# Two-layer transformer on one core: GpSimd adds the attention masks for two steps in one operation, VectorE adds none

## The chip, the cores and the metric

One core of one Trainium2 chip. The metric is the device time of one execution in microseconds, as the median of several runs.

## The reference

x is 4 x 512 x 256 (B = 4 sequences). Layer 0 is a conditioned transformer block with 16 heads of width 16, an additive bias of 4 x 16 x 512 x 512 values in f32 (64 MB, the largest input) and a mask; layer 1 is a causal block with a gate. The part that the change touches:

```
scores = jnp.einsum('bhqd,bhkd->bhqk', q / math.sqrt(HEAD_DIM), k)
scores = scores + attention_bias
scores = jnp.where(src_mask, -jnp.inf, scores.astype(jnp.float32))
probs = jax.nn.softmax(scores, axis=-1).astype(v.dtype)
ctx = jnp.einsum('bhqk,bhkd->bhqd', probs, v)
```

## The kernel before

The work is written out by hand for each engine, with semaphores. Phases alternate: X(b) is the attention of layer 0 for sequence b+1 (b = -1 to 2), Y(b) that of layer 1 for sequence b. Beside each runs "dense" work (projections, feed-forward, norms) from other sequences, put in at slots that the table PLANS (L83) gives. In the trace X(-1) runs from about 45 to 147 us, X0 from 147 to 273, X1 from 374 to 495, X2 from 600 to 723.

A phase X has 64 steps, one for each head and query tile. Each step has a tile of 128 x 512 f32 in a ring of 12 (`tiles`, RING). Its life:

- SyncE loads the bias into it, `load_tile` (L385), once TensorE has read the tile of 12 steps before.
- The mask is added in place: `tile += mask_neg[:, t, :]`, where mask_neg (bf16, 128 x 4 x 512) holds one row block for each query tile t = `tile_of(s)[1]` and is rewritten for each sequence by VectorE, `turn_mask` (L1234), after all mask adds of the sequence before. GpSimd adds it, `add_mask` (L565, L572), 6 steps ahead (MASK_AHEAD). In the first phase, every fourth step is VectorE's instead (`masked_by_vector` L181, `add_mask` L1378, L1382), 16 steps in all.
- TensorE puts q.k into PSUM (L958), three steps ahead (AHEAD). VectorE adds it to the tile and takes the row maximum in one instruction, `add_bias` (L1384, L1391).
- The maximum is subtracted, by ScalarE (L696) or, every eighth step, by VectorE (`from_max`, L1398).
- TensorE transposes the tile (`turn`, L966), ScalarE takes the exponential (L705), TensorE multiplies with v (L979).

Steps 2i and 2i + 1 are the two query tiles t and t + 1 of one head, with t even, so their tiles lie side by side in the ring and their mask rows side by side in mask_neg.

GpSimd runs in order: in a phase X one mask at each slot, and behind it what falls due in that slot: `inv_std` (L575, L577: waits for VectorE's var_eps, then a power), row adds of 128 x 1024 (`add_row`, L580), and, in the first phase, a reordering of weights (L561). A norm goes: VectorE's statistics and var_eps (L1222), GpSimd's inv_std, VectorE's normalised tiles (`normalise`, L1292, four of 128 x 256; or `modulate`, L1300 and L1304), TensorE's transposes (`transposed`), which wait for them tile by tile. q and k are split into three bf16 parts by VectorE (`split`: L1358, L1362, L1365) and moved by DMA into the order of the scores (`to_roles`, L413). `gated` (L1342) is L1346 and L1348; L1348 frees a bank of PSUM for TensorE's feed-forward (L932). In phase Y GpSimd cuts diagonals (L611) and adds the first six masks of the next sequence but one (`first_masks`, L640); VectorE's `split_max` is L1416 to L1422.

Of the kernel before, what the change touches and what calls it, by code (L numbers as in the profile page):

```python
# [19 lines left out]
ALU = mybir.AluOpType  # L20
# [4 lines left out]
B, S, D = 4, 512, 256  # L25
# [28 lines left out]
STEPS = H * T  # L54
# [3 lines left out]
RING = 12  # L58
AHEAD = 3
MASK_AHEAD = 6  # L60
# [93 lines left out]
def s_no(l, b, i):  # L154
    return STEPS * place(l, b) + i
# [19 lines left out]
def tile_of(s):  # L175

    part, j = s // (2 * G), s % (2 * G) // 2
    return part // 2 * G + j, part % 2 * 2 + s % 2


def masked_by_vector(b, s):  # L181
    return b == 0 and s % 4 == 1


def masks(b, s, vector):

    return sum(masked_by_vector(c, i) == vector for c in range(b + 1) for i in range(s + 1 if c == b else STEPS))


def shifted_by_vector(s):  # L190
    return s % 8 == 3

# [32 lines left out]
def all_upto(streams, slot):  # L225
    for stream in streams:
        stream.upto(slot)


def the_rest(streams, slot):  # L230
    for s in range(slot, slot + 40):
        all_upto(streams, s)
    all_upto(streams, LAST)


def two_layers(nc, a, out):
# [21 lines left out]
    with ExitStack() as ctx:  # L258
        def sb(name, shape, dt=F32):
            return ctx.enter_context(nc.sbuf_tensor(name, shape, dt))  # L260
# [4 lines left out]
        def sem(name):  # L265
            return ctx.enter_context(nc.semaphore(name))
# [15 lines left out]
        mask_neg = sb("mask_neg", [P, T, S], BF16)  # L282
# [14 lines left out]
        tiles = sb("tiles", [P, RING, S])  # L297
# [44 lines left out]
        def tile(b, s):  # L342
            return tiles[:, (b * STEPS + s) % RING, :]
# [7 lines left out]
        w1_in, w2_in, wq_scaled = sem("w1_in"), sem("w2_in"), sem("wq_scaled")  # L351
        x_in, mask_in, mask_ready = [sem(f"x_in{b}") for b in range(B)], sem("mask_in"), sem("mask_ready")
        tile_in = [sem(f"tile_in{i}") for i in range(RING)]
        masked_p, masked_v, shifted_a, shifted_v = (sem(n) for n in ("masked_p", "masked_v", "shifted_a", "shifted_v"))
        s_filled, s_drained, e_filled, e_done = (sem(n) for n in ("s_filled", "s_drained", "e_filled", "e_done"))
        pv_done, raw_ready, raw_turned, ctx_normed, ctx_turned, ctx_ready = (sem(n) for n in (
            "pv_done", "raw_ready", "raw_turned", "ctx_normed", "ctx_turned", "ctx_ready"))
# [186 lines left out]
        def _(pool):  # L544
# [11 lines left out]
            def swap_columns(l):  # L556

                pool.wait_ge(qk_in[l], 16 * 2)
                for x, (w, scale) in enumerate(((wq, QSCALE), (wk, 1.0))):
                    yield 12 + 4 * x  # L560
                    pool.tensor_scalar(w[l][:, :, :].rearrange("p c (n d h) -> p (c n) d h", n=C, d=DH),  # L561
                                       raw[l][:, x, :, :].rearrange("p c (n h d) -> p (c n) d h", n=C, d=DH),
                                       scale, None, ALU.mult).then_inc(wq_scaled, 1)

            def add_mask(b, s):  # L565
                if masked_by_vector(b, s):
                    return
                n = b * STEPS + s
                if s == 0:
                    pool.wait_ge(mask_ready, b + 1)  # L570
                pool.wait_ge(tile_in[n % RING], 16 * (n // RING + 1))
                pool.tensor_tensor(tile(b, s), tile(b, s), mask_neg[:, tile_of(s)[1], :], ALU.add).then_inc(masked_p, 1)  # L572

            def inv_std(l, b, which):
                n = NORMS.index((l, b, which))  # L575
# [29 lines left out]
            def diagonal(b, h):  # L605

                pool.wait_ge(e_done, e_no(1, b, CHUNKS * (h + 1)))
                at = h % KEEP * P1
                for blocks in (prob[:, at:at + 2048].rearrange("p (i n) -> p i n", i=2)[:, :, 0:P],
                               prob[:, at + 512:at + 768].rearrange("p (i n) -> p i n", i=2)):  # L610
                    pool.affine_select(out=blocks, in_=blocks, compare_op=ALU.is_ge, fill=0.0, base=0,  # L611
                                       pattern=[[0, 2], [1, P]], channel_multiplier=-1).then_inc(diagonal_done, 1)
# [23 lines left out]
            def residual(b, at):  # L636
                yield at.x1
                set_x1(b)

            def first_masks(b, at):  # L640
                for s in range(MASK_AHEAD if b < B else 0):
                    yield at.masks + 2 * s
                    add_mask(b, s)

            def streams(at):
                return [Stream(second_norm(at)), Stream(projections(at))]
# [5 lines left out]
            inv_std(0, 0, 0)  # L652

            pool.wait_ge(norm_ready, T)
            for s in range(MASK_AHEAD):
                add_mask(0, s)
            def first_bo():
                yield 8
                add_bo(0)

            for kind, b in PHASES:
                dense = streams(PLANS[kind, b])
                if kind == "X":
                    if b < 0:
                        dense += [Stream(first_bo()), Stream(swap_columns(1))]
                    for s in range(STEPS):
                        if s + MASK_AHEAD < STEPS:
                            add_mask(b + 1, s + MASK_AHEAD)
                        all_upto(dense, s)
                    the_rest(dense, STEPS)  # L670
                    if b < 0:
                        for s in range(MASK_AHEAD):
                            add_mask(1, s)
                else:
                    dense += [Stream(residual(b, PLANS[kind, b])), Stream(first_masks(b + 2, PLANS[kind, b]))]
                    for slot in range(Y_SLOTS):
                        u, i = divmod(slot, 4)
                        if u >= LAG and i == 3:
                            diagonal(b, u - LAG)
                        all_upto(dense, slot)  # L680
                    the_rest(dense, Y_SLOTS)
# [504 lines left out]
        def _(dve):  # L1186
# [46 lines left out]

            def turn_mask(b, last):  # L1234
                if b:
                    dve.wait_ge(masked_p, masks(b - 1, STEPS - 1, False))
                    dve.wait_ge(masked_v, masks(b - 1, STEPS - 1, True))
                dve.wait_ge(v_step, last)
                for t in range(T):
                    ins = dve.tensor_scalar(mask_neg[:, t, :], mask_u8[:, t, :], -BIG, mask_row[:, 2, t:t + 1], ALU.mult, ALU.add)  # L1240
                ins.then_inc(mask_ready, 1)
# [133 lines left out]
                                  bv_all[l][:, :].rearrange("p (h d) -> p h d", d=DH).unsqueeze(1).to_broadcast([P, 2, H, DH]),  # L1375
                                  ALU.add).then_inc(drained_v, 1)

            def add_mask(b, s):  # L1378
                n = b * STEPS + s
                dve.wait_ge(mask_ready, b + 1)  # L1380
                dve.wait_ge(tile_in[n % RING], 16 * (n // RING + 1))
                dve.tensor_tensor(tile(b, s), tile(b, s), mask_neg[:, tile_of(s)[1], :], ALU.add).then_inc(masked_v, 1)  # L1382

            def add_bias(b, s):  # L1384
                n = s_no(0, b, s)
                if masked_by_vector(b, s):
                    dve.wait_ge(masked_v, masks(b, s, True))
                else:
                    dve.wait_ge(masked_p, masks(b, s, False))
                dve.wait_ge(s_filled, n + 1)  # L1390
                dve.tensor_tensor_reduce(tile(b, s), psS[:, n % 2, :], tile(b, s), 1.0, -3e38, ALU.add, ALU.max,  # L1391
                                         rmax[0][:, s:s + 1]).then_inc(s_drained, 1)

            def from_max(b, s):
                if not shifted_by_vector(s):
                    return
                dve.wait_ge(s_drained, s_no(0, b, s) + 1)
                dve.tensor_scalar(tile(b, s), tile(b, s), rmax[0][:, s:s + 1], -1.0, ALU.subtract, ALU.mult).then_inc(shifted_v, 1)  # L1398
# [106 lines left out]
            def phase_x(b, dense):  # L1505
                for s in range(-AHEAD, STEPS):
                    if 0 <= s + AHEAD < STEPS:
                        if s < 0 and masked_by_vector(b + 1, s + AHEAD):
                            add_mask(b + 1, s + AHEAD)
                        add_bias(b + 1, s + AHEAD)  # L1510
                    if 0 <= s + AHEAD - 1 < STEPS:
                        from_max(b + 1, s + AHEAD - 1)
                    if s >= 0 and s + AHEAD + 1 < STEPS and masked_by_vector(b + 1, s + AHEAD + 1):
                        add_mask(b + 1, s + AHEAD + 1)
                    if s >= 4 * G and s % (4 * G) == 8:
                        divide_by_sums(0, b + 1, s // (4 * G) - 1)
                    if s >= 0:
                        all_upto(dense, s)
                the_rest(dense, STEPS)
# [57 lines left out]
```

## Time and profile before

| | us |
|---|---|
| median of 3 runs | 988.09 |
| lowest, highest | 975.78, 990.17 |
| profiled execution | 990.58 |
| its span | 988.7 |
| mean granted TensorE clock | 0.926 |
| POOL L572, 240 mask adds | 283.4 busy, 1205 ns each |
| DVE L1382, 16 mask adds | 16.2 busy, 1010 ns each |
| DVE L1391, 256 biases with maximum | 174.3 busy, 688 ns each |

The profile is of one execution. PE is TensorE, DVE VectorE, ACT ScalarE, POOL GpSimd; L is a line of the kernel. An instruction's time begins when its waits on semaphores are over, so time that it stands for another reason is part of its duration. Where several instructions are merged into a row, its time is that from the first start to the last end.

### The profile page before, as it was taken

What the parts mean: (1) busy time and instruction counts of PE and PEld (TensorE: products, weight loads), DVE (VectorE), ACT (ScalarE), POOL (GpSimd) and SP (SyncE); (2) the same over time, 40 slices, a digit from 0 to 9 for tenths busy, and PEclk for the clock granted to TensorE, in tenths of its full rate; (3) what the DMA queues carried; (4) which work ended last, traced back from release to release, by engine and by line L of the source; (5) the groups of instructions that cost most, each with busy time, mean ns of one, the idle gap of its engine ahead of it and who ended that gap; (6) DMA issues with size and microseconds to landing.
All of it is one profiled execution on the core that took longest, in us unless ns stands there. A gap on an engine that the chain in (4) does not pass through costs nothing.

```text
span 988.7 us, 14633 instructions
## 1 busy us (share of the span) xinstructions
PE 827.4 (84%) x4856; PEld 494.6 (50%) x4856; DVE 599.9 (61%) x1693; ACT 493.0 (50%) x879; POOL 410.1 (41%) x421
## 2 busy tenths in 40 slices
PE   6778888789866879898998887899999898698778
PEld 2354456458542334575645443566656363445345
DVE  6599874774738936656847854656836654636021
ACT  1257785756701357577732455666742435054421
POOL 4377558755302447486302536486501123012320
PEclk7779999999976899999998997999999999899879
DMA  8776976434570036356741037455631126100000
GB/s 249 154 234 192 249 252 186 140 117 129 158 162 1 1 65 163 105 182 202 207 114 44 2 98 165 123 171 183 157 66 44 44 65 139 33 1 5 19 1 22
DMA packets 80045, 114.74 MB, mean 116 GB/s; under 512 B 7691, under 2 KB 43359, under 8 KB 79971
## 3 DMA queue, kind: packets, MB, share of 16 engines
q1 hardware_dynamic: 79971, 113.81, 41.8%
q8 instruction: 39, 0.64, 0.3%
q14 instruction: 35, 0.29, 0.1%
HBM read 86.33 MB, written 2.10 MB: 89 GB/s over the span
## 4 chain that ended last, share of the span: by engine, by line
PE 59%; DVE 19%; issue 8%; ACT 7%; DMA 3%; SPq 2%; POOL 1%; DVEq 0%; ACTq 0%; POOLq 0%
PE psD L932 11%; PE psD L944 11%; PE psE L966 6%; PE psC L979 5%; PE psD L904 4%; PE psC L1024 4%; PE psS L958 4%; PE psD L920 3%; DVE tiles L1391 3%; DMA qk<-work 2%; ACT tiles L696 2%; ACT prob L705 2%; DVE junk L1406 2%; PE psS L994 2%; PE psD L911 2%
## 5 line engine op out<-in xcount | busy, mean ns | idle before, releaser
L572 POOL TENSOR_TENSOR tiles<-tiles,mask_neg 128x512 f32<-128x512 f32 x240 | 283.4, 1205 | 97.3 <-DMA tiles<-in_fside_Bx16xSxS 79.4
L1391 DVE CUSTOM_DVE_ANT_0 tiles<-psS,tiles 128x512 f32<-128x512 f32 x256 | 174.3, 688 | 143.5 <-PE psS L958 129.9
L705 ACT ACTIVATE prob<-psE 128x512 f32<-128x512 f32 x256 | 150.9, 595 | 102.2 <-PE psE L966 94.6
L696 ACT ACTIVATE tiles<-tiles,rmax 128x512 f32<-128x512 f32 x224 | 161.4, 722 | 61.4 <-DVE rmax L1391 60.8
L966 PE MATMUL psE<-ident,tiles 128*128 128x128 f32 x1024 | 162.3, 282 | 7.7 <-ACT prob L705 7.3
L966 PEld LDWEIGHTS psE<-ident,tiles 128*128 128x128 f32 x1024 | 130.3, 145 | 63.5 <-ACT prob L705 25.0
L932 PE MATMUL psD<-hT,w 128*128 128x512 f32 x256 | 131.9, 627 | 17.4 <-DVE work L1348 13.6
L944 PE MATMUL psD<-w,work 128*128 128x256 f32 x512 | 133.8, 386 | 6.0 <-ACT hT L748 4.8
L1406 DVE CUSTOM_DVE_ANT_0 junk<-psS,later 128x128 bf16<-128x128 f32 x192 | 82.7, 444 | 86.4 <-PE psS L994 85.9
L611 POOL TENSOR_SCALAR_AFFINE_SELECT prob<-prob 128x256 f32<-128x256 f32 x128 | 52.4, 433 | 190.2 <-ACT prob L717 190.2
L958 PE MATMUL psS<-qk 96*128 96x512 bf16 x256 | 102.6, 403 | 31.9 <-DVE rmax L1391 20.6
L717 ACT ACTIVATE prob<-psE 128x512 f32<-128x512 f32 (+1 forms) x144 | 72.9, 532 | 90.2 <-PE psE L1012 89.4
L577 POOL TENSOR_TENSOR rstd<-var_eps,neg_half 128x4 f32<-128x4 f32 x16 | 16.5, 1033 | 226.8 <-DVE var_eps L1222 226.7
L944 PEld LDWEIGHTS psD<-w,work 128*128 128x128 f32 x512 | 92.0, 193 | 21.4 <-ACT hT L748 6.0
L994 PE MATMUL psS<-qk 96*128 96x128 bf16 x192 | 54.3, 296 | 28.0 <-DVE rmax L1406 18.0
L932 PEld LDWEIGHTS psD<-hT,w 128*128 128x128 f32 x256 | 44.8, 198 | 56.2 <-issue 33.7
L979 PE MATMUL psC<-prob,vx 128*32 128x256 f32 x1024 | 65.4, 399 | 1.0 <-ACT prob L705 1.0
L1406 DVE CUSTOM_DVE_ANT_0 junk<-psE,later 128x384 bf16<-128x384 f32 x64 | 39.4, 621 | 38.7 <-PE psE L994 38.6
L958 PEld LDWEIGHTS psS<-qk 96*128 96x128 bf16 x256 | 25.3, 99 | 65.4 <-DVE rmax L1391 32.3
L1024 PE MATMUL psC<-prob,vx 128*32 128x128 f32 (+3 forms) x512 | 48.4, 529 | 4.8 <-POOL prob L611 4.8
L1012 PE MATMUL psE<-qk 99*128 99x512 bf16 (+1 forms) x192 | 48.4, 306 | 2.4 <-DMA qk<-mT 1.5
L777 ACT ACTIVATE work<-psD,cols 128x512 f32<-128x512 f32 x32 | 22.0, 687 | 54.0 <-PE psD L932 54.0
(119 smaller groups left out, 1038.4 us busy)
## 6 DMA issues: line engine op xcount, KB each, us to landing
tiles<-in_fside_Bx16xSxS SPq DMA_DIRECT2D x256, 256.0 KB, 2.9
qk<-work SPq DMA_DIRECT2D x96, 256.0 KB, 5.8
w<-in_L_cond_W SPq DMA_DIRECT2D x12, 1024.0 KB, 5.5
res<-in_x SPq DMA_DIRECT2D x4, 512.0 KB, 4.8
out<-x SPq DMA_DIRECT2D x4, 512.0 KB, 2.8
mask_u<-in_mask_Bx1xSxS_bk SPq DMA_DIRECT2D x4, 256.0 KB, 5.5
qk<-mT SPq DMA_DIRECT2D x64, 3.0 KB
prob<-in_L_cond_W_ada SPq DMA_DIRECT2D x1, 512.0 KB
```

What stands on the lines that cost most here:

```text
L572: pool.tensor_tensor(tile(b, s), tile(b, s), mask_neg[:, tile_of(s)[1], :], ALU.add).then_inc(masked_p, 1)
L696: act.activation(tile(b, s), tile(b, s), ACT.Identity, scale=-1.0, bias=rmax[0][:, s:s + 1]).then_inc(shifted_a, 1)
L705: act.activation(prob0[:, part_no % 2, j, :, s % 2 * P:(s % 2 + 1) * P], psE[:, e_no(0, b, s) % 2, :].rearrange("p (k q) -> p k q", k=T), ...
L932: mm = pe.matmul(psD[:, n % 2, :], w1[:, c, f * P:(f + 1) * P], hT2[:, c, :], start=c == 0, stop=c == C - 1)
L944: mm = pe.matmul(psD[:, n % 2, t % 2 * D:(t % 2 + 1) * D], gT[:, f, t * P:(t + 1) * P], w2[:, f, :], start=f == 0, stop=f == FC - 1)
L958: pe.matmul(psS[:, n % 2, :], q6[0:ROWS, h, t * P:(t + 1) * P], k6[0:ROWS, h, :], start=True, stop=True).then_inc(s_filled, 1)
L966: mm = pe.transpose(psE[:, n % 2, kt * P:(kt + 1) * P], tile(b, s)[:, kt * P:(kt + 1) * P], ident[:, :])
L979: mm = pe.matmul(psC[j * QW:(j + 1) * QW, half * S // 2:(half + 1) * S // 2], vx[0][:, kt, at:at + QW], prob0[:, part_no % 2, j, kt, :], s ...
L994: pe.matmul(s_bank(n, i)[:, 0:(t + 1) * P], q6[0:ROWS, h, t * P:(t + 1) * P], k6[0:ROWS, h, 0:(t + 1) * P], start=True, stop=True).then_in ...
L1024: mm = pe.matmul(psC[j * QW:(j + 1) * QW, kt * P:S], vx[1][:, kt, VW * h:VW * h + QW], prob1[:, h % KEEP, P1_AT[kt]:P1_AT[kt] + S - kt * P ...
L1391: dve.tensor_tensor_reduce(tile(b, s), psS[:, n % 2, :], tile(b, s), 1.0, -3e38, ALU.add, ALU.max, rmax[0][:, s:s + 1]).then_inc(s_drained, 1)
L1406: dve.tensor_tensor_reduce(junk[:, n % 2, 0:w], s_bank(n, h * T + t)[:, 0:w], later[:, S - w:S], 1.0, -3e38, ALU.add, ALU.max, rmax[1][:, ...
```

## The change

VectorE's mask adds and their bookkeeping (`masked_by_vector`, `masks`, two semaphores) go. GpSimd's `add_mask(b, s)` becomes `add_masks(b, s)`, called for even s alone: it waits for both tiles of the pair and adds both masks in one operation of 128 x 2 x 512. One semaphore, `masked`, counts pairs; VectorE's bias waits for the count of its pair. Each pair is issued at the slot at which its first step's mask was issued.

```diff
-def masked_by_vector(b, s):
-    return b == 0 and s % 4 == 1
...
-            def add_mask(b, s):
-                if masked_by_vector(b, s):
-                    return
+            def add_masks(b, s):
+
                 n = b * STEPS + s
                 if s == 0:
                     pool.wait_ge(mask_ready, b + 1)
-                pool.wait_ge(tile_in[n % RING], 16 * (n // RING + 1))
-                pool.tensor_tensor(tile(b, s), tile(b, s), mask_neg[:, tile_of(s)[1], :], ALU.add).then_inc(masked_p, 1)
+                for i in range(2):
+                    pool.wait_ge(tile_in[(n + i) % RING], 16 * (n // RING + 1))
+                two, t = tiles[:, n % RING:n % RING + 2, :], tile_of(s)[1]
+                pool.tensor_tensor(two, two, mask_neg[:, t:t + 2, :], ALU.add).then_inc(masked, 1)
...
             def first_masks(b, at):
-                for s in range(MASK_AHEAD if b < B else 0):
+                for s in range(0, MASK_AHEAD if b < B else 0, 2):
                     yield at.masks + 2 * s
-                    add_mask(b, s)
+                    add_masks(b, s)
...
-            for s in range(MASK_AHEAD):
-                add_mask(0, s)
+            for s in range(0, MASK_AHEAD, 2):
+                add_masks(0, s)
...
                     for s in range(STEPS):
-                        if s + MASK_AHEAD < STEPS:
-                            add_mask(b + 1, s + MASK_AHEAD)
+                        if s % 2 == 0 and s + MASK_AHEAD < STEPS:
+                            add_masks(b + 1, s + MASK_AHEAD)
                         all_upto(dense, s)
...
                 if b:
-                    dve.wait_ge(masked_p, masks(b - 1, STEPS - 1, False))
-                    dve.wait_ge(masked_v, masks(b - 1, STEPS - 1, True))
+                    dve.wait_ge(masked, STEPS // 2 * b)
...
             def add_bias(b, s):
                 n = s_no(0, b, s)
-                if masked_by_vector(b, s):
-                    dve.wait_ge(masked_v, masks(b, s, True))
-                else:
-                    dve.wait_ge(masked_p, masks(b, s, False))
+                dve.wait_ge(masked, (STEPS * b + s) // 2 + 1)
...
             def phase_x(b, dense):
                 for s in range(-AHEAD, STEPS):
                     if 0 <= s + AHEAD < STEPS:
-                        if s < 0 and masked_by_vector(b + 1, s + AHEAD):
-                            add_mask(b + 1, s + AHEAD)
                         add_bias(b + 1, s + AHEAD)
                     if 0 <= s + AHEAD - 1 < STEPS:
                         from_max(b + 1, s + AHEAD - 1)
-                    if s >= 0 and s + AHEAD + 1 < STEPS and masked_by_vector(b + 1, s + AHEAD + 1):
-                        add_mask(b + 1, s + AHEAD + 1)
```

## Rows read from the trace of the kernel before

**Rows 1.** The page, part 1: busy time, share, instructions
```profile
PE 827.4 (84%) x4856; PEld 494.6 (50%) x4856; DVE 599.9 (61%) x1693; ACT 493.0 (50%) x879; POOL 410.1 (41%) x421
```

**Rows 2.** Windows: stretch, length, busy of PE, PEld, DVE, ACT, POOL, clock, DMA
```profile
45.00:150.00 105.00, 85.35 (x595) 52.19 (x594) 89.99 (x200) 75.90 (x134) 63.76 (x49) 0.91 0.79 232
385.00:500.00 115.00, 103.58 (x738) 69.70 (x736) 77.36 (x196) 78.78 (x134) 66.45 (x56) 1.00 0.59 177
```

**Rows 3.** The chain that ended last, 45 to 150 us, share by line
```profile
by line: ACT tiles L696 13.4%; issue 13.2%; ACT prob L705 9.9%; DVE tiles L1382 7.4%; DVE tiles L1391 6.4%; PE psE L966 5.9%; PE psD L904 5.4%; PE psC L979 5.3%; DVE res L1300 5.3%; PE psS L958 5.0%; DVE tiles L1398 3.4%; POOL tiles L572 3.
```

**Rows 4.** Groups by shape: busy us, mean ns, idle time before
```profile
L572 POOL TENSOR_TENSOR tiles<-tiles,mask_neg 128x512 f32<-128x512 f32 x240 | 283.4, 1205 | 97.3 <-DMA tiles<-in_fside_Bx16xSxS 79.4 <-DVE mask_neg L1240 7.9 <-DVE res L1304 7.5
L580 POOL TENSOR_TENSOR res<-res,b_all 128x1024 f32<-128x1024 f32 x4 | 9.4, 2352 | 7.3 <-DVE xh L1292 7.3
L1382 DVE TENSOR_TENSOR tiles<-tiles,mask_neg 128x512 f32<-128x512 f32 x16 | 16.2, 1010 | 0.0
```

**Rows 5.** Line L572: duration min/median/max in ns; who waited for it
```profile
L572 POOL TENSOR_TENSOR tiles<-tiles,mask_neg x240: 1143/1158/1617, 23.2 to 709.0; 128x512 f32<-128x512 f32 x120
...
  DVE tiles L1391: 12.9, 14
```

**Rows 6.** Groups of VectorE by shape
```profile
L1365 DVE TENSOR_TENSOR work<-work 128x512 bf16<-128x512 f32 x32 | 26.6, 832 | 0.4
L1398 DVE TENSOR_SCALAR tiles<-tiles,rmax 128x512 f32<-128x512 f32 x32 | 25.5, 798 | 0.0
...
L1292 DVE TENSOR_SCALAR xh<-res,mv,rstd 128x256 f32<-128x256 f32 x32 | 19.9, 663 | 1.1 <-POOL rstd L577 1.1
L1346 DVE TENSOR_SCALAR work<-work 128x512 f32<-128x512 f32 x32 | 19.3, 602 | 0.0
...
L1362 DVE CAST work<-work 128x512 bf16<-128x512 f32 x32 | 17.8, 556 | 0.4
...
L1300 DVE SCALAR_TENSOR_TENSOR res<-res,mv,ada 128x256 f32<-128x256 f32 x16 | 10.9, 720 | 1.5 <-ACT ada L755 1.3
```

**Rows 7.** Two lines of VectorE, ns min/median/max
```profile
L1292 DVE TENSOR_SCALAR xh<-res,mv,rstd x32: 402/452/1258, 180.6 to 817.9; 128x256 f32<-128x256 f32 x32
...
L1398 DVE TENSOR_SCALAR tiles<-tiles,rmax x32: 482/712/1458, 50.1 to 716.2; 128x512 f32<-128x512 f32 x32
```

**Rows 8.** Order of time at the start: start us, us
```profile
29.86 0.43 DVE L1362 CAST work<-work 128x512 bf16<-128x512 f32 x1
30.19 5.57 POOL L572 TENSOR_TENSOR tiles<-tiles,mask_neg 128x512 f32<-128x512 f32 x4 [2.46 <-DMA res<-in_L_cond_Wk]
...
30.33 1.56 DVE L1365 TENSOR_TENSOR work<-work 128x512 bf16<-128x512 f32 x1
...
33.22 1.53 DVE L1365 TENSOR_TENSOR work<-work 128x512 bf16<-128x512 f32 x1
...
37.93 0.69 DVE L1365 TENSOR_TENSOR work<-work 128x512 bf16<-128x512 f32 x1
```

**Rows 9.** Order of time, modulation: undisturbed, then in the first phase
```profile
19.67 0.88 DVE L1300 SCALAR_TENSOR_TENSOR res<-res,mv,ada 128x256 f32<-128x256 f32 x2 [1.01 <-ACT ada L755]
...
59.78 3.54 DVE L1300 SCALAR_TENSOR_TENSOR res<-res,mv,ada 128x256 f32<-128x256 f32 x2 [0.25 <-ACT ada L755]
63.35 2.55 DVE L1304 SCALAR_TENSOR_TENSOR res<-res,rstd,ada 128x256 f32<-128x256 f32 x2
```

**Rows 10.** Order of time around the norm in X1
```profile
459.60 0.71 DVE L1398 TENSOR_SCALAR tiles<-tiles,rmax 128x512 f32<-128x512 f32 x1
...
460.85 1.82 DVE L1292 TENSOR_SCALAR xh<-res,mv,rstd 128x256 f32<-128x256 f32 x2
...
463.20 1.80 DVE L1292 TENSOR_SCALAR xh<-res,mv,rstd 128x256 f32<-128x256 f32 x2
...
458.87 11.62 POOL L572 TENSOR_TENSOR tiles<-tiles,mask_neg 128x512 f32<-128x512 f32 x10
```

**Rows 11.** The chain at the start of X0: start us, us
```profile
145.55 3.39 POOL tiles L572 x3
```

More of the change, by code:

```diff
@@ L178, in tile_of @@
     return part // 2 * G + j, part % 2 * 2 + s % 2
-def masked_by_vector(b, s):
-    return b == 0 and s % 4 == 1
-def masks(b, s, vector):
-    return sum(masked_by_vector(c, i) == vector for c in range(b + 1) for i in range(s + 1 if c == b else STEPS))
 def shifted_by_vector(s):
@@ L353, in two_layers @@
         tile_in = [sem(f"tile_in{i}") for i in range(RING)]
-        masked_p, masked_v, shifted_a, shifted_v = (sem(n) for n in ("masked_p", "masked_v", "shifted_a", "shifted_v"))
+        masked, shifted_a, shifted_v = (sem(n) for n in ("masked", "shifted_a", "shifted_v"))
         s_filled, s_drained, e_filled, e_done = (sem(n) for n in ("s_filled", "s_drained", "e_filled", "e_done"))
@@ L671, in _ @@
                     if b < 0:
-                        for s in range(MASK_AHEAD):
-                            add_mask(1, s)
+                        for s in range(0, MASK_AHEAD, 2):
+                            add_masks(1, s)
                 else:
@@ L1376, in keep_values @@
                                   ALU.add).then_inc(drained_v, 1)
[L1378 to L1382, printed above, removed]
             def add_bias(b, s):
                 n = s_no(0, b, s)
-                if masked_by_vector(b, s):
-                    dve.wait_ge(masked_v, masks(b, s, True))
-                else:
-                    dve.wait_ge(masked_p, masks(b, s, False))
+                dve.wait_ge(masked, (STEPS * b + s) // 2 + 1)
                 dve.wait_ge(s_filled, n + 1)
```

## The prediction

> **What bounds the kernel now.** I read the page first, for the engines' shares: TensorE is busy for 827 of 989 us, VectorE for 600, GpSimd for 410 [rows 1]. So no engine's total is the limit by itself, and the stages have to be read apart. The windows over two phases X (layer 0's attention, the only place where masks are added) show two regimes [rows 2]. In the first one, 45 to 150 us, VectorE is busy for 90 of 105 us and GpSimd for 64; TensorE has 20 us of gaps. In a later one, 385 to 500 us, TensorE is busy for 104 of 115 us, VectorE for 77, GpSimd for 66. The chain of work in the first phase [rows 3] passes through ScalarE (L696 and L705, 23%) and VectorE; VectorE's own mask adds, L1382, are 7.4% of these 105 us, 7.8 us. Third come the groups of GpSimd and VectorE by shape [rows 4, 6], for the price of each operation, and last the order in time at the places where both engines work at once [rows 8 to 11].
>
> **What the rows show of the two engines side by side.** L1398, whose shortest run is 482 ns, takes up to 1458 [rows 7]. 1458 less the 300 ns that are left of it is one mask add of 1158 [rows 5]: the instruction stood until GpSimd's was over, then ran. L1300 takes 0.44 us undisturbed (two in 0.88, rows 9) and 1.77 each where a 2.35 us GpSimd add lies over them [rows 9]. L1292, L1346, L1362, L1365, L1300 and L1304 show the same; L1391, which reads PSUM, keeps to its time. When GpSimd has a backlog the two take turns: in X1 four L1292 take 1.82 + 1.80 us beside ten adds in a row of 11.62 us [rows 10]. From means less the undisturbed duration this costs VectorE: L1398 32 x (798-482) = 10.1 us, L1292 32 x (663-402) = 8.4, L1346 32 x (602-430) = 5.5 (floor as L1362's, of the same width), L1365 32 x (832-690) = 4.5, L1362 32 x (556-430) = 4.0, L1300 16 x (720-440) = 4.5: 37 us, of which mask adds are the greater part [rows 6 to 9].
>
> **The change part by part.**
> *Price of a pair.* Before shows no 128x1024 add of f32 and bf16. Nearest: the one-tile add, 1205 ns in the mean, 1158 median [rows 4, 5], so 2.32 to 2.41 a pair, and L580, as wide with two f32 inputs, 2352 [rows 4]. I take 2.35. 2 x 1158 is 2316, so nothing is saved by joining. [...]
> *GpSimd's load.* 240 singles become 128 pairs: 283.4 us become 128 x 2.35 = 301. All 17 us fall in the first phase (64 to some 81 of 105 us); elsewhere it is unchanged. GpSimd waits there for tiles and for norms, so this hides; without cover it would be 17 us.
> *VectorE's sixteen L1382 go*: 16.2 us at 1010 ns [rows 4], all in the first phase. On the chain are 7.8 of them [rows 3]; ScalarE's two lines stand right behind, so I credit the chain's share: **-7.8** (bounds -16.2, all of it, and -4, if ScalarE takes the place in half).
> *The start.* GpSimd's first masks lie beside the four splits of q and k, which end in the load that the first scores wait for. Before, two L1365 take 1.56 and 1.53 instead of 0.69 [rows 8]. After, pairs run 23.2-25.6-27.9-30.3-32.6-35.0-37.3 without a gap (the wait for Wk, 2.46 us, falls under the third). L1362 at 29.86 stands until 30.3, L1365 until 32.6, the next L1362 until 35.0, and L1365 until 37.3: the second split ends at 37.6 instead of 34.75, and this is serial: **+2.9** (bounds 0 and 3.2).
> *First phase, modulation.* The pairs of L1300 and L1304 take 3.54 and 2.55 us instead of 0.88 each, one GpSimd operation over each [rows 9]. One of these operations is 2.35 long already, the others are masks. With pairs each of the others is up to 1.2 longer; two or three of them count. Add the splits and L1398 of the phase. I take **+4** (bounds 0 and +9, three quarters of a doubling of what L1300, L1304, L1365, L1362 and L1398 lose there).
> *Start of X0.* mask_neg is rewritten, and steps 0 to 2 wait for GpSimd one add each, 3.39 us on the chain [rows 11]. After, step 0 waits for 2.35 and the third tile for the second pair, 4.7: **+1.2**.
> *The norms inside the phases.* inv_std frees both engines at once: GpSimd starts on the masks that it held back, VectorE on L1292. This happens four times (two norms in X0, one each in X1 and X2; L1292's largest is 1258 for a floor of 402, rows 7). X1, walked through: pairs from 458.87 end at 461.2, 463.6, 465.9. L1398 at 459.60 stands until 461.2, a bias step follows, the first L1292 ends at 463.9, the second at 466.2, a bias step, the last two near 469; before they ended at 465.0 [rows 10]: +4. TensorE's transposes wait for exactly these, and it is the full engine there. The same walk gives +1.5 at X0's first norm, where two pairs are ready and then L580 waits itself for L1292; +3 at its second, with three pairs; and +1.7 in X2, where the fourth pair's tiles have not landed. Sum **+10** (bounds 0 and 13).
> *L1346, L1398, L1362 and L1365 in X0 to X2.* A wait met at random grows from half of 1.16 us to half of 2.35. These lose about 16 us there now, so 16 more in all; L1346 stands ahead of the operation that frees TensorE's bank (L1348), the others have two steps of slack. I put a fifth on the path: **+3.5** (bounds 0 and 16).
> *Mask latency.* The first tile of a pair is ready one tile's arrival and 1.2 us later. Before, only 14 of 256 steps waited for a mask, 12.9 us in all [rows 5], nearly all counted above. 0. The last phases and phase Y have few masks, beside split_max: **+1**. Semaphores: two waits on tile_in before each pair instead of one before each single, same count.
>
> Sum: -7.8 + 2.9 + 4 + 1.2 + 10 + 3.5 + 1 = **+14.8**. The profiled execution took 990.6 us and would take 1005; it lies 2.5 above the median of 988.1, so against the median I predict **1003 us**.
>
> **The rivals.**
> *Relief wins (the other side).* If TensorE's and ScalarE's queues absorb the longer stands, the norms' +10 and the +3.5 vanish, since L1391 has idle time before it in every phase, and the first phase keeps its -7.8: 988.1 - 7.8 + 2.9 + 4 + 1.2 + 1 = 989; with all 16.2 of L1382 and no loss by turns, 972. For it: VectorE is busy for only 61% of the span. Against: the L1292 stand right before the transposes of a TensorE that is 90% busy. It decides from where the four norm places lose under 2 us together.
> *The turns cost in full.* If each of the 37 us doubles and all is on the path, in place of the +4, +10 and +3.5: 988.1 - 7.8 + 2.9 + 1.2 + 37 + 1 = 1022. Against: L1398's wait appears in front of nobody for long, and an engine in order with idle time gives some back.
> *GpSimd lets VectorE in between the two halves of a pair.* Then a stand is as before, and the sum is 988.1 - 7.8 + 1.2 = 982. Against: L1300 stood through a 2.35 us add as one piece [rows 9]. The Trainium skill (SBUF — State Buffer, section "SBUF: two separate sides") says the shared port pair is held for a whole instruction; this trace agrees, 1.77 us each where 0.44 is the floor.
> *Masks come late.* If each of the 14 waits grows by the 1.2 us of the second tile, that is +17 beside the sum: 1020. Against: load, mask and use are several steps apart; for it: the first tiles after each norm are taken at once.
>
> **How the numbers follow.** Chances: the forecast, 994 to 1012, 0.50; relief wins, 980 to 993, 0.25; between the halves, 0.03; turns in full, 1012 to 1022, 0.15; masks late, 0.07. Range 980 to 1018: it leaves out about 0.1 above and the 0.05 below. Two per cent, about what can be told from no change, is 19.8 us: slower than 1007.9 has the rivals above, 0.22 less a little, and a tenth of the forecast: 0.30. Faster than 968.3 needs all of L1382 and a faster run besides: 0.04. The rest, 0.66.
>
> **What would show it.** In the profile after: the pair at 2.35 us with 128 of them; GpSimd at about 427 us busy; L1382 gone; mean L1398 near 1.1 us and L1292 (from res) near 1.0, with maxima of 2.65; the first scores near 47.5 instead of 44.6; at the four norms TensorE waiting for L1292 by 2 to 4 us more. It is wrong if the L1292 and L1398 maxima stay at 1.26 and 1.46, if a pair is far from 2.35, or if VectorE waits for L572 far beyond 12.9 us.

## The result and the profile after

| | before | after |
|---|---|---|
| median, us (lowest to highest, 4 runs each) | 985.41 (975.78 to 990.17) | 1006.54 (1001.87 to 1009.11) |
| profiled execution, its span | 990.58, 988.7 | 1007.85, 1006.1 |

(The 988.09 us given ahead of the prediction are the median of the first three of these four runs.) The changed kernel is slower: ratio 1.0214, 95% interval 1.016 to 1.0267, so about 21 us. That is clear of no change, though the interval does not clear 2%. Ratios compare only the runs within 1.5% of a kernel's fastest, medians are of all its runs, so the two can differ a little. Between the two profiled executions it is 17.3 us. The line numbers move: GpSimd's add is now L564, the bias L1373, from_max L1380, normalise L1283, gated L1337 and L1339, split L1353 and L1356.

The page after, part 1, the line that answers to [rows 1]:

```profile
PE 837.5 (83%) x4856; PEld 501.4 (50%) x4856; DVE 614.8 (61%) x1677; ACT 494.6 (49%) x879; POOL 403.4 (40%) x309
```

TensorE has the same 4856 matmuls and is busy for 10 us more (827.4 before); its mean granted clock is 0.919 instead of 0.926. VectorE has 16 instructions less and is busy for 15 us more (599.9 before). GpSimd has 112 instructions less and is busy for 7 us less. So GpSimd's sum fell, VectorE's own work fell by 16 us, and its busy time rose all the same. The groups by shape say where (busy us, mean ns | idle time before), beside [rows 4, 6]:

```profile
L564 POOL TENSOR_TENSOR tiles<-tiles,mask_neg 128x1024 f32<-128x1024 f32 x128 | 276.5, 2177 | 114.5 <-DMA tiles<-in_fside_Bx16xSxS 102.7 <-DVE res L1295 6.0 <-DVE mask_neg L1231 5.8
...
L1373 DVE CUSTOM_DVE_ANT_0 tiles<-psS,tiles 128x512 f32<-128x512 f32 x256 | 174.3, 687 | 140.8 <-PE psS L950 133.3 <-POOL tiles L564 6.9
L1380 DVE TENSOR_SCALAR tiles<-tiles,rmax 128x512 f32<-128x512 f32 x32 | 38.1, 1192 | 0.0
L1356 DVE TENSOR_TENSOR work<-work 128x512 bf16<-128x512 f32 x32 | 27.8, 869 | 0.4
...
L1283 DVE TENSOR_SCALAR xh<-res,mv,rstd 128x256 f32<-128x256 f32 x32 | 25.4, 836 | 1.1 <-POOL rstd L569 1.1
...
L1337 DVE TENSOR_SCALAR work<-work 128x512 f32<-128x512 f32 x32 | 23.8, 742 | 0.0
...
L1353 DVE CAST work<-work 128x512 bf16<-128x512 f32 x32 | 21.2, 661 | 0.4
```

from_max went from 798 to 1192 ns in the mean, normalise from 663 to 836, gated's first operation from 602 to 742, split's cast from 556 to 661. The bias, which reads PSUM, stayed at 688 and 687. The standing is the time that an instruction takes beyond its floor, the duration that it has undisturbed. With the floors of the prediction the standing of the six groups named there rose from 37 to 65 us (32 x 710 + 32 x 434 + 32 x 312 + 32 x 179 + 32 x 231 + 16 x 326 ns). VectorE waited less for masks than before (6.9 us, 12.9 in [rows 5]).

Single lines, ns min/median/max, beside [rows 5, 7]: the largest stand grew by 0.84 us (1458 to 2302 ns), the add by 0.98.

```profile
L564 POOL TENSOR_TENSOR tiles<-tiles,mask_neg x128: 2120/2137/2569, 22.6 to 723.3; 128x1024 f32<-128x1024 f32 x128
```
```profile
L1380 DVE TENSOR_SCALAR tiles<-tiles,rmax x32: 475/1400/2302, 51.2 to 731.8; 128x512 f32<-128x512 f32 x32
```

Where the time went is read from the bias steps of each phase, first and last start in us: L1391 of before, windows on the four phases X,

```profile
L1391 DVE CUSTOM_DVE_ANT_0 tiles<-psS,tiles x64: 673/691/693, 45.4 to 143.2; 128x512 f32<-128x512 f32 x64
L1391 DVE CUSTOM_DVE_ANT_0 tiles<-psS,tiles x64: 674/691/693, 146.8 to 267.8; 128x512 f32<-128x512 f32 x64
L1391 DVE CUSTOM_DVE_ANT_0 tiles<-psS,tiles x64: 672/691/693, 374.1 to 491.6; 128x512 f32<-128x512 f32 x64
L1391 DVE CUSTOM_DVE_ANT_0 tiles<-psS,tiles x64: 673/691/693, 600.0 to 719.5; 128x512 f32<-128x512 f32 x64
```

and L1373 of after:

```profile
L1373 DVE CUSTOM_DVE_ANT_0 tiles<-psS,tiles x64: 672/691/692, 47.2 to 143.9; 128x512 f32<-128x512 f32 x64
L1373 DVE CUSTOM_DVE_ANT_0 tiles<-psS,tiles x64: 673/691/693, 148.4 to 270.3; 128x512 f32<-128x512 f32 x64
L1373 DVE CUSTOM_DVE_ANT_0 tiles<-psS,tiles x64: 674/691/693, 377.6 to 504.3; 128x512 f32<-128x512 f32 x64
L1373 DVE CUSTOM_DVE_ANT_0 tiles<-psS,tiles x64: 673/691/693, 611.9 to 734.4; 128x512 f32<-128x512 f32 x64
```

The lag, after less before at the same step, is 1.8 us at the first bias and 0.7 at the end of the first phase: the relief and the losses there nearly cancel. X0 takes it to 2.5, X1 from 3.5 to 12.7, X2 from 11.9 to 14.9. X1 is the largest single piece, 9.2 us, and it is made of two things: VectorE's stands, and TensorE's clock behind them. The first growth, 1.1 us, is a stand away from any norm. A pair starts as soon as its tiles have landed, and gated's first operation starts 0.12 us behind it and takes 2.30 us, where the same one took 1.24 before (order of time, start us, us; first VectorE, then GpSimd):

```profile
400.93 2.30 DVE L1337 TENSOR_SCALAR work<-work 128x512 f32<-128x512 f32 x1
```
```profile
400.81 2.14 POOL L564 TENSOR_TENSOR tiles<-tiles,mask_neg 128x1024 f32<-128x1024 f32 x1 [1.04 <-DMA tiles<-in_fside_Bx16xSxS]
```

Over the next steps, 16 to 19, the lag grows by 2.25 us more, from 4.8 to 7.0. One L1337 stands for 0.6 us there; the rest goes with the clock. Windows of before and of after over these same steps, and of the stretch at 1.2 GHz inside the second (stretch, length, busy of PE, PEld, DVE, ACT, POOL, clock, DMA):

```profile
404.69:411.10 6.41, 4.82 (x23) 2.65 (x22) 4.46 (x11) 3.60 (x7) 0.31 (x1) 1.00 0.31 84
```
```profile
409.47:418.13 8.66, 6.50 (x23) 3.35 (x22) 5.03 (x12) 3.61 (x7) 1.32 (x1) 0.80 0.23 67
412.60:416.00 3.40, 3.40 (x9) 1.57 (x7) 1.30 (x3) 1.21 (x2) 0.00 (x0) 0.50 0.07 19
```

The same 23 matmuls take 4.82 us before and 6.50 after. The granted clock fell to 1.2 GHz at 412.6, after ten microseconds in which TensorE had been busy for 6.4; in before it stayed at 2.4 GHz over the same steps. The inv_std at 420 then releases two pairs at once, and L1380 and L1337 take 1.96 and 1.75 us beside them (0.98 and 0.65 before), but this puts only 0.5 us on the lag (7.0 to 7.5).

The other place is the norm that the prediction walked through [rows 10]:

```profile
467.09 1.70 DVE L1380 TENSOR_SCALAR tiles<-tiles,rmax 128x512 f32<-128x512 f32 x1
...
469.31 1.94 DVE L1283 TENSOR_SCALAR xh<-res,mv,rstd 128x256 f32<-128x256 f32 x2
...
471.78 4.21 DVE L1283 TENSOR_SCALAR xh<-res,mv,rstd 128x256 f32<-128x256 f32 x2
```
```profile
466.36 4.42 POOL L564 TENSOR_TENSOR tiles<-tiles,mask_neg 128x1024 f32<-128x1024 f32 x2
471.59 4.25 POOL L564 TENSOR_TENSOR tiles<-tiles,mask_neg 128x1024 f32<-128x1024 f32 x2 [0.81 <-DMA tiles<-in_fside_Bx16xSxS]
```

The second two normalised tiles take 4.21 us instead of 1.80, two whole pairs. Counted from var_eps (457.63 before, 465.12 after) the last one ends 3.5 us later than before. The lag grows by 4.0 us up to step 48, and by 1.0 more up to step 50, while the clock is at 1.2 GHz (474.0 to 480.8). Windows over steps 44 to 50, before, then after:

```profile
459.00:469.99 10.99, 9.06 (x76) 5.80 (x74) 7.97 (x19) 8.36 (x14) 10.99 (x10) 1.00 0.65 220
```
```profile
466.48:482.45 15.97, 11.67 (x76) 7.18 (x74) 11.52 (x18) 8.47 (x14) 10.10 (x5) 0.79 0.45 146
```

So the clock is part of the loss in the profiled execution. From the mean clocks of the two, TensorE was at 1.2 GHz for an estimated 146 us of before and 163 us of after (1 less the mean clock, times two, times the span). In the two places shown, the drop follows a stretch in which TensorE had waited; that the stands caused it is likely from this order of events, but no run shows it by itself.

### The profile page after: what moved, and what is told of

It reads as the page before. It is cut to its first block, busy times and chain, and to the rows that moved or that the text cites. A ratio compares the mean times of both kernels' runs of the same rounds, so it can differ in the third digit from the quotient of the medians.

```text
span 1006.1 us, 14613 instructions
## 1 busy us (share of the span) xinstructions
PE 837.5 (83%) x4856; PEld 501.4 (50%) x4856; DVE 614.8 (61%) x1677; ACT 494.6 (49%) x879; POOL 403.4 (40%) x309
## 4 chain that ended last, share of the span: by engine, by line
PE 59%; DVE 20%; issue 8%; ACT 6%; DMA 3%; SPq 2%; POOL 1%; DVEq 0%; ACTq 0%; POOLq 0%
PE psD L924 11%; PE psD L936 11%; PE psE L958 7%; PE psS L950 4%; PE psC L971 4%; PE psD L896 4%; PE psC L1016 4%; PE psD L912 3%; DVE tiles L1373 3%; PE psD L903 2%; DMA qk<-work 2%; DVE junk L1388 2%; PE psS L986 2%; DVE xh L1283 2%; PE psD L882 2%
## 5 line engine op out<-in xcount | busy, mean ns | idle before, releaser
L564 POOL TENSOR_TENSOR tiles<-tiles,mask_neg 128x1024 f32<-128x1024 f32 x128 | 276.5, 2177 | 114.5 <-DMA tiles<-in_fside_Bx16xSxS 102.7
L1373 DVE CUSTOM_DVE_ANT_0 tiles<-psS,tiles 128x512 f32<-128x512 f32 x256 | 174.3, 687 | 140.8 <-PE psS L950 133.3
L958 PE MATMUL psE<-ident,tiles 128*128 128x128 f32 x1024 | 163.9, 284 | 10.8 <-ACT prob L697 9.2
```

Of the source, the lines that this page charges most:

```text
L564: pool.tensor_tensor(two, two, mask_neg[:, t:t + 2, :], ALU.add).then_inc(masked, 1)
L958: mm = pe.transpose(psE[:, n % 2, kt * P:(kt + 1) * P], tile(b, s)[:, kt * P:(kt + 1) * P], ident[:, :])
```

## The experiments

The theory ("hold"): the VectorE operations named above, which read and write SBUF alone, stand until GpSimd's running one is over, and a pair nearly doubles the time for which it runs (1158 to 2137 ns). Rivals: "load" (GpSimd has 16 masks more in the first phase), "mask latency" (the first tile of a pair is ready later). The rival that the traces add is the clock: after's four runs had a mean granted clock of 0.919 to 0.928, the 49 recorded runs of before 0.918 to 0.944. Each ratio below is to the kernel before, run beside it on the same chip.

**1. Singles, all by GpSimd.**

```diff
 def masked_by_vector(b, s):
-    return b == 0 and s % 4 == 1
+    return False
```

> The kernel before, with the sixteen mask adds of VectorE in the first phase given to GpSimd as single adds of 128x512; no pairs. If the longer hold of a pair is what cost time (theory 'hold'), this kernel is not slower: VectorE loses 16.2 us of work and meets singles only, 980 to 988 us, and from X0 on it is like before. If it is GpSimd's greater load in the first phase ('load'), this carries all of that and shows most of the loss: about 1000.

984.37 us, ratio 0.9948 (0.9923 to 0.9973). GpSimd's load of the first phase is carried here in full (301.4 us of mask adds) and the kernel is slightly faster than before, so "load" is out, and the relief of VectorE is worth half a per cent net.

**2. Two singles in place of a pair.**

```diff
+                for i in range(2):
+                    ins = pool.tensor_tensor(tile(b, s + i), tile(b, s + i), mask_neg[:, tile_of(s + i)[1], :], ALU.add)
+                    ins.then_inc(masked, 1)
-                two, t = tiles[:, n % RING:n % RING + 2, :], tile_of(s)[1]
-                pool.tensor_tensor(two, two, mask_neg[:, t:t + 2, :], ALU.add).then_inc(masked, 1)
```

The waits of VectorE count twice as far.

> The changed kernel, but add_masks issues two adds of 128x512, one after the other, in place of one of 128x1024. Order, waits for both tiles and the pair's semaphore count stay as in the changed kernel. 'Hold': VectorE gets in between the two, so most of the loss is gone: 985 to 993 us, L1292 of X1 and X2 back under 1.3 us. 'Mask latency' (the first tile of a pair is ready later) or 'load': it stays near 1005.

991.45 us, ratio 1.002 (0.998 to 1.006). Order, waits and the moment at which VectorE may go on are those of the changed kernel; only that each pair is two GpSimd operations instead of one differs, and 1.9 of the 2.1% are gone by the ratios, 15 us by the medians. The granted clock does not account for it: it was 0.911 to 0.927 in this kernel's runs, as low as in the changed kernel's. from_max and the bias in this kernel, groups by shape:

```profile
L1374 DVE CUSTOM_DVE_ANT_0 tiles<-psS,tiles 128x512 f32<-128x512 f32 x256 | 174.2, 688 | 158.0 <-PE psS L951 126.2 <-POOL tiles L564 31.3
...
L1381 DVE TENSOR_SCALAR tiles<-tiles,rmax 128x512 f32<-128x512 f32 x32 | 22.2, 694 | 0.0
```

from_max is back at 694 ns. VectorE now waits for masks, 31.3 us against 16.3 in kernel 1. The distance between kernels 1 and 2 is 0.7%. It may be the price of the later mask of a pair, but it comes together with a lower clock, 0.921 in the mean against 0.932. In the 49 recorded runs of the kernel before, 0.01 of clock goes with some 7.4 us (a straight line through them), so that an estimated 8 us would go with this difference alone; what lowered the clock is open. So the change in parts, by ratios: -0.5% relief, +1.9% hold, and +0.7% that goes with the order of the pairs and is not explained further. The first and the last are each near the width of their intervals; the hold is not.

**3 and 4. GpSimd waits at six norms** until the four tiles are normalised, in the changed kernel and in the one before.

```diff
                 pool.tensor_tensor(rstd[:, :], var_eps[:, :], neg_half[:, :], ALU.pow).then_inc(rstd_ready, 1)
+                if (l, b, which) in ((0, 0, 1), (1, 0, 0), (1, 0, 1), (1, 1, 0), (1, 1, 1), (1, 2, 0)):
+                    pool.wait_ge(norm_ready, T * (n + 1))
```

> The changed kernel, and GpSimd, after inv_std of the six norms inside X0, X1 and X2 that end in L1292, waits until the four tiles are normalised before it goes on with masks. 'Hold' has half of the loss at these places: L1292 falls to 0.41 us each, and the time to 994 to 1000. If the norms are not where it is lost, it stays at 1006 or rises by the delay of the masks (up to +4).

1015.26 us, ratio 1.0258 (1.0192 to 1.0325).

> The kernel before with the same wait at the six norms. Singles cost less there: 'hold' gives 2 to 7 us, 981 to 986 of 988, the delayed masks could eat that. If masks get late, 990 or more.

1002.94 us, ratio 1.0142 (1.01 to 1.0183). Kernel 3 lies above every range given for it; kernel 4 fell where the expectation put late masks, and further out. normalise did fall to its floor, but the masks came late, in kernel 3 too (34.6 us of waiting for them); kernel 4, groups by shape:

```profile
L1393 DVE CUSTOM_DVE_ANT_0 tiles<-psS,tiles 128x512 f32<-128x512 f32 x256 | 174.7, 688 | 146.7 <-PE psS L960 110.1 <-POOL tiles L572 35.6
...
L1294 DVE TENSOR_SCALAR xh<-res,mv,rstd 128x256 f32<-128x256 f32 x32 | 11.7, 412 | 1.1 <-POOL rstd L577 1.1
```

The wait for masks grew from 12.9 to 35.6 us while the standing of L1292 that it removed was 8 us. GpSimd's backlog after a norm is itself wanted soon; it cannot be put off by the 4 us that a norm takes. Late masks are not all of it in kernel 4: one from_max there stood for 5.84 us, in a row of eleven adds of 128x512 without a gap (its line's min/median/max, then order of time, VectorE and GpSimd):

```profile
L1400 DVE TENSOR_SCALAR tiles<-tiles,rmax x32: 481/622/5840, 49.6 to 718.1; 128x512 f32<-128x512 f32 x32
```
```profile
670.63 5.84 DVE L1400 TENSOR_SCALAR tiles<-tiles,rmax 128x512 f32<-128x512 f32 x1
```
```profile
663.86 12.33 POOL L572 TENSOR_TENSOR tiles<-tiles,mask_neg 128x512 f32<-128x512 f32 x11
```

**5. Half tiles:** kernel 1 with two adds of 128x256 for each tile.

```diff
+                for x in range(2):
+                    half = slice(x * S // 2, (x + 1) * S // 2)
+                    ins = pool.tensor_tensor(tile(b, s)[:, half], tile(b, s)[:, half], mask_neg[:, tile_of(s)[1], half], ALU.add)
+                    ins.then_inc(masked_p, 1)
-                pool.tensor_tensor(tile(b, s), tile(b, s), mask_neg[:, tile_of(s)[1], :], ALU.add).then_inc(masked_p, 1)
```

> GpSimd adds all masks, each tile's in two adds of 128x256: the hold is half of a single's, the number of operations is four times that of the pairs, and GpSimd's total grows by about 0.18 us for each extra operation (2 x 1158 - 2137), 46 us. 'Hold': VectorE's stands shrink further (L1398 under 0.7 in the mean instead of 0.75) and the time is 980 to 985 where singles gave 984, unless GpSimd's total makes masks late in the first phase; then up to 992. If only the number of handovers counted, it would be worse than pairs, above 1006.

1009.68 us, ratio 1.018, with a wide interval (1.0011 to 1.0348): the four runs spread from 995.79, the profiled one, to 1016.6. The median is where I had put "only the number of handovers counts". This goes against "hold" as I had put it, and the trace says why. from_max by shape, its line's min/median/max, and one of its places in order of time (VectorE, then GpSimd):

```profile
L1400 DVE TENSOR_SCALAR tiles<-tiles,rmax 128x512 f32<-128x512 f32 x32 | 54.7, 1709 | 0.0
```
```profile
L1400 DVE TENSOR_SCALAR tiles<-tiles,rmax x32: 480/538/10822, 47.4 to 721.5; 128x512 f32<-128x512 f32 x32
```
```profile
100.11 10.82 DVE L1400 TENSOR_SCALAR tiles<-tiles,rmax 128x512 f32<-128x512 f32 x1
```
```profile
98.71 11.94 POOL L574 TENSOR_TENSOR tiles<-tiles,mask_neg 128x256 f32<-128x256 f32 x19
```

The median is 538 ns, as short holds should give. But five of the 32 stood for 5.8 to 10.8 us, beside an unbroken row of GpSimd adds, and ended as the row ended. TensorE waited for from_max for 17.8 us in all. Here the two engines did not take turns. So the length of one operation is not all; a row of short ones can shut VectorE out altogether. With singles of 1.16 us this is rarer: the one of kernel 4 is the only such case in the traces of the kernels with singles (largest L1398 1458 before, 1477 in kernel 1). GpSimd's sum also rose, to 340.5 us, from 301.4 in kernel 1.

**6. Four tiles in one add,** from the changed kernel, issued eight steps ahead.

```diff
-                two, t = tiles[:, n % RING:n % RING + 2, :], tile_of(s)[1]
-                pool.tensor_tensor(two, two, mask_neg[:, t:t + 2, :], ALU.add).then_inc(masked, 1)
+                four = tiles[:, n % RING:n % RING + 4, :].rearrange("p (j i) k -> p j (i k)", i=2)
+                t = tile_of(s)[1]
+                rows = mask_neg[:, t:t + 2, :].rearrange("p i k -> p (i k)").unsqueeze(1).to_broadcast([P, 2, 2 * S])
+                pool.tensor_tensor(four, four, rows, ALU.add).then_inc(masked, 1)
```

> Four tiles in one add of 128x2048 (some 4.1 us), issued eight steps ahead. 'Hold' carried on from singles to pairs (+15 to +20 us a doubling): L1398 beyond 1.8 us in the mean, 1020 to 1045 us, part of it by masks that come late, to be read from L1391's wait for the mask. If hold is not the cause, near 1000.

1070.29 us, ratio 1.09 (1.079 to 1.101), beyond my range. The add takes 4105 ns:

```profile
L566 POOL TENSOR_TENSOR tiles<-tiles,mask_neg 128x2048 f32<-128x2048 f32 x64 | 262.4, 4105 | 253.4 <-DMA tiles<-in_fside_Bx16xSxS 238.4 <-DVE mask_neg L1233 8.2 <-DVE res L1297 6.9
...
L1382 DVE TENSOR_SCALAR tiles<-tiles,rmax 128x512 f32<-128x512 f32 x32 | 60.6, 1893 | 0.0
```

GpSimd's mask time is the least of all kernels that add masks, 262 us, and the kernel is the slowest. GpSimd now sits idle for 238 us until tiles land: with four tiles of twelve tied together the ring is a bound of its own. How much of the 9% is that and how much the hold was not separated.

**7 and 8. Eight steps ahead** instead of six (`MASK_AHEAD = 8`), in kernel 1 and in the changed kernel.

> All masks by GpSimd as singles, issued eight steps ahead instead of six. GpSimd then does two more masks in the time in which it waits for a norm's var_eps, so fewer are left to collide with L1292. 'Hold': 1 to 4 us less than the 984 of six ahead. If the norms' collisions do not matter, 984; if GpSimd waits for tiles that have not landed and inv_std comes late, 988.

987.65 us, ratio 1.004 (0.9988 to 1.0092).

> The changed kernel with pairs issued eight steps ahead. 'Hold': a pair less to collide at each norm, 2 to 6 us less than 1006. Otherwise 1006, or more where inv_std is late behind a tile that has not landed.

1009.46 us, ratio 1.0252 (1.0129 to 1.0375). No gain in either. In kernel 8 normalise fell to 555 ns in the mean, as meant, and from_max rose to 1432: the collisions moved to another operation.

```profile
L1380 DVE TENSOR_SCALAR tiles<-tiles,rmax 128x512 f32<-128x512 f32 x32 | 45.8, 1432 | 0.0
...
L1283 DVE TENSOR_SCALAR xh<-res,mv,rstd 128x256 f32<-128x256 f32 x32 | 16.4, 555 | 1.1 <-POOL rstd L569 1.1
```

**9. No masks.** Both engines' adds left out, the bias waits for the tile's load.

```diff
             def add_mask(b, s):
-                if masked_by_vector(b, s):
-                    return
+                return
...
-                if masked_by_vector(b, s):
-                    dve.wait_ge(masked_v, masks(b, s, True))
-                else:
-                    dve.wait_ge(masked_p, masks(b, s, False))
+                dve.wait_ge(tile_in[(b * STEPS + s) % RING], 16 * ((b * STEPS + s) // RING + 1))
```

> The kernel before without any mask add: GpSimd's and VectorE's are both left out, the bias step waits for the tile's load alone (so masked keys are not masked). It measures what all mask adds cost on the path, relief and turns together. 'Hold': more than VectorE's own 8 us come back, 965 to 975 of 988, and L1292, L1398, L1346 fall to their floors. If the masks were hidden and only VectorE's sixteen cost time: 980.

961.88 us, ratio 0.9724 (0.9658 to 0.9789). It is below the 965 to 975 that I had expected of "hold". The masks cost 2.8% in the kernel before, though GpSimd is busy for only 41% of it; the changed kernel pays 4.9 points. from_max and normalise stand at their floors:

```profile
L1391 DVE TENSOR_SCALAR tiles<-tiles,rmax 128x512 f32<-128x512 f32 x32 | 15.4, 482 | 0.0
L1288 DVE TENSOR_SCALAR xh<-res,mv,rstd 128x256 f32<-128x256 f32 x32 | 11.7, 411 | 1.1 <-POOL rstd L576 1.1
```

**10. Pairs, and every subtraction of the maximum by ScalarE** (`shifted_by_vector` returns False).

> The changed kernel with VectorE's 32 subtractions of the maximum (L1380, 1192 ns in the mean, 22 us of it standing) given to ScalarE (32 x 0.72 us more there). If these stands are on the path, 997 to 1002 of 1006; if they are off it and ScalarE's load takes their place, 1006 to 1012.

1002.25 us, ratio 1.0112 (1.0057 to 1.0166). By the ratios half of the change's loss goes with VectorE's 32 operations, by the medians (1006.54 and 1002.25, taken beside different runs of before) a fifth, in spite of 23 us more for ScalarE. So their standing is on the path in part, some 4 to 10 us.

**11. Pairs from the second sequence on,** the first phase as before.

```diff
+                if b:
+                    if s % 2 == 0:
+                        for i in range(2):
+                            pool.wait_ge(tile_in[(n + i) % RING], 16 * (n // RING + 1))
+                        two, t = tiles[:, n % RING:n % RING + 2, :], tile_of(s)[1]
+                        pool.tensor_tensor(two, two, mask_neg[:, t:t + 2, :], ALU.add).then_inc(masked_p, 1)
+                    return
```

> The kernel before in the first phase (singles, VectorE's sixteen), pairs as in the changed kernel for the sequences 1 to 3. The trace puts +0.7 us of the change into the first phase and the rest behind it. So about 1004, at least 1.5% above before. If the loss came from the first phase after all (start, load, modulation), 990.

1006.76 us, ratio 1.0166 (1.0104 to 1.0228). Most of the loss is there without any change to the first phase, in line with the lags of the bias steps.

**12. Kernel 1 with holds at X0's two norms** (the diff of 3 with its first two entries alone).

> All masks by GpSimd as singles (984) and, at the two norms of X0 alone, GpSimd waits until the four tiles are normalised. The run with holds at six norms gained 4.8 us in X0 by its trace and lost them in X1 and X2, where masks came late. So 979 to 981; if that gain was only a shift that is given back at the next wait, 984 or more.

985.27 us, ratio 0.997 (0.9917 to 1.0023). Not to be told from kernel 1: whatever the holds gain in X0 does not last to the end. Kernel 1 remains the fastest that computes everything, 0.5% below the kernel before.

## Why the prediction was right

The likeliest time was 1003 and the measured one 1006.5, and the main mechanism named, VectorE standing for as long as one GpSimd operation lasts, is the one that the runs show. That the sum came so close is in part luck: some terms were too large, one was too small, and TensorE's clock was not among them. By its steps:

- **The stand until GpSimd's operation is over.** Right. Kernel 2 changes this alone and takes 1.9 of 2.1% back; kernel 9 removes it and finds the floors. One reading behind it was loose: in [rows 9] the two L1300 did not take 1.77 us each. The view of that line gives 1.38 and 2.24, the second beside the 2.35 us add, and a floor of 0.48 (two records overlap in 0.88). The point holds by the second one.

```profile
L1300 DVE SCALAR_TENSOR_TENSOR res<-res,mv,ada x2: 1380/1808/2235, 59.8 to 61.9; 128x256 f32<-128x256 f32 x2
```

- **Price of a pair.** 2.35 was too high; it is 2137 in the median, 2177 in the mean. 2 x 1158 less 2137 is 179 ns saved by joining, where the prediction had nothing. The nearest row had two f32 inputs, this one has f32 and bf16, and the row's own 512-wide form was not in the trace: I compared the width of one operation with that of another. GpSimd's total was 403 instead of 427 us for the same reason.
- **VectorE's sixteen adds, -7.8, start +2.9, modulation +4.** Together -0.9 at the end of the first phase; measured +0.7. The start alone was +1.8. L1353 and L1356 stood for 2.35 and 2.49 us, but the next pair ran out a little sooner than walked. So the relief and the modulation together gave back 1.1, not the 3.8 of the sum.
- **Start of X0, +1.2.** The lag grew from 0.7 to 1.6 at the first bias, but was 0.9 from step 5 on: +0.2 that lasted.
- **The norms, +10.** X1's walked one put 4.0 on the lag of the bias steps, as worked out. X0's first put on 0.9 (1.5 worked out; gone four steps later, where before has a stretch at 1.2 GHz of its own, 187.0 to 190.4), its second 2.1 (3), X2's 0.9 (1.7). That is 7.9 directly. Behind X0's second and X1's the lag grew by another 1.7 and 1.0 over stretches at 1.2 GHz.
- **L1346, L1398 and splits, +3.5.** This is the term that was mis-sized. I took random meetings, doubled, with a fifth on the path. L1398 (L1380) met a pair in 21 of its 32 places, with a median of 1400 ns where 712 was before, and its standing rose from 10.1 to 22.7 us, more than double. Right behind an inv_std lie six of these stands, 6.7 us; twelve, 12.3 us, lie beside pairs that had started when their tiles landed. Why it meets those so often was not looked into. Kernel 10 puts L1380's part at 4 to 10 us, though it also shifts what the others meet. One stand of L1337 in X1 put 1.1 us on the lag by itself.
- **TensorE's clock, not in the sum.** Between the two profiled executions the same matmuls took 10 us more of TensorE's time. Over all runs, after's mean clock was 0.9225 and before's 0.932 (in the runs that its ratios count); by the 7.4 us for each 0.01 this is an estimated 7 of the 21 us. It overlaps with the pieces of the lag named here, and it may follow from the stands.
- **Mask latency, 0.** The visible wait fell to 6.9 us, yet kernels 1 and 2 differ by 0.7%, with more waiting for masks in kernel 2 and a lower clock. Which of the two costs the time is open. The rival "masks come late" was real in kernels 3 and 4.
- **The last phases, +1.** From the end of X2 the lag grew by 2.4, over Y2, where no mask is added. The windows show the granted clock there at 0.97 after and 0.99 before, so this piece may belong to the single execution and not to the change.

"Relief wins" fell: the four norms lost 7.9 us, not under 2. (The chance for slower than 1007.9 adds up to at most 0.27 from its own parts, not 0.30.) "VectorE gets in between the two halves" fell by L1380's largest, 2302 ns.

## What to carry to other kernels

In these traces a GpSimd add that reads and writes SBUF also held up the VectorE operations that read and write SBUF alone, and not those that read PSUM (the bias: 688 and 687 ns). Joining two adds saved 0.18 us on GpSimd and made each hold 0.98 us longer. Before joining, look for VectorE's lines whose maximum is far above their minimum, and for the places where both engines are set going by the same event, such as a norm or a tile that lands. Then look at the clock behind them: where TensorE had waited, its granted clock fell for the steps that followed in the two places shown here. A mask add on an engine that is 40% busy was not free: all of them together cost 2.8%, and only leaving them out showed it.

## What was not expected of the hardware

Turns are not guaranteed. In the trace of kernel 5 a VectorE operation of 482 ns stood for 10.82 us beside GpSimd adds of 128x256 in an unbroken row, and four more stood for 5.8 to 8.3 us, while normalise in the same kernel had a mean of 587. In kernel 4 one stood for 5.84 us beside five adds of 128x512, a length beside which VectorE got in after one or two operations everywhere else, in before through a row of ten [rows 10]. What decides between the two was not settled.

The mask adds of the kernels give the price of a GpSimd add of f32 and bf16: 671 ns in the median at 256 columns, 1158 at 512, 2137 at 1024 and 4080 at 2048. These lie near a straight line, an estimated 1.9 ns for each column and 0.18 to 0.2 us for each instruction. The add of two f32 inputs at 1024 columns took 2352 ns [rows 4], a tenth more than the 2137 of f32 and bf16.
